# VectorE's rotation of the next query split in two, with the mask and the carry of the states between its cosine and its sine products

## What is computed

```
q = rope(x wq), k = rope(x wk), v = x wv          # 16 query heads, 4 key heads, 128 wide, batch 2
rope(t) = t * cos + rot(t) * sin                  # rot swaps the halves of a head
scores = (q k^T) * diag                           # within a block, with decay exp(-lam * distance)
o      = scores v + (q * q_dec) state             # what earlier blocks add, through the state
state  = blk * state + (k * k_dec)^T v            # carried from block to block
x      = x + (o wo)
```

## Time and profile before

| | us |
|---|---|
| median of 3 runs | 578.29 |
| lowest and highest | 576.17, 578.62 |
| the profiled execution | 576.15 (span of its core 574.5) |

### The profile page before, as it was taken

One profiled execution on the slowest core, in us unless ns is written; L12 is line 12 of the kernel. 1 busy time (PEld: TensorE's weight loads), 2 busy tenths in 40 slices (PEclk: granted clock), 3 DMA queues, 4 the chain that ended last, 5 costly groups with the idle time before them and its releaser, 6 DMA issues.

```text
span 574.5 us, 10574 instructions
## 1 busy us (share of the span) xinstructions
PE 503.9 (88%) x3560; PEld 449.3 (78%) x3560; DVE 337.2 (59%) x974; ACT 153.6 (27%) x381; POOL 290.3 (51%) x312
## 2 busy tenths in 40 slices
PE   8689999999378999899999999999878999999900
PEld 7589988886357989799989988889777898888700
DVE  6844444443367898977767868676674444444417
ACT  4102222222332233333233322332310222222211
POOL 0045666664337566557555645555004566666332
PEclk9879999999588999999999999999977999999965
DMA  7989997873722331212121212211495422877455
GB/s 232 331 255 314 347 335 278 286 244 109 251 93 66 92 111 56 67 54 84 51 78 50 81 56 83 61 51 47 135 343 181 140 93 92 293 261 238 144 207 192
DMA packets 54722, 93.10 MB, mean 162 GB/s; under 512 B 7424, under 2 KB 37376, under 8 KB 54656
## 3 DMA queue, kind: packets, MB, share of 16 engines
q1 hardware_dynamic: 45440, 71.29, 38.0%
q0 software_dynamic: 6912, 18.88, 10.0%
q10 hardware_dynamic: 2304, 2.10, 1.1%
HBM read 79.67 MB, written 12.58 MB: 161 GB/s over the span
## 4 chain that ended last, share of the span: by engine, by line
PE 69%; DVE 15%; issue 6%; DMA 6%; POOL 2%; ACT 1%; SPq 0%; DVEq 0%; ACTq 0%; POOLq 0%
PE bank L1196 11%; PE bank L1191 8%; PE bank L1291 7%; PE bank L1342 7%; PE bank L1215 5%; PE bank L1217 5%; PE bank L1324 4%; PE bank L1302 4%; PE bank L1313 3%; PE bank L1330 3%; PE bank L1163 3%; DVE x_sb L982 3%; PE bank L1256 2%; DMA shared<-z_dram 2%; PE bank L1206 1%
## 5 line engine op out<-in xcount | busy, mean ns | idle before, releaser
L492 POOL DMA_INDIRECT decay_all<-xn_dram,ids x72 | 69.6, 966 | 113.7 <-PE bank L1163 46.3
L938 DVE COPY oT_all<-bank 128x256 f32<-128x256 f32 x72 | 30.6, 425 | 126.2 <-PE bank L1163 126.2
L501 POOL DMA_INDIRECT z_dram<-probs_all,dest x72 | 70.2, 974 | 36.5 <-ACT probs_all L691 32.8
L564 POOL TENSOR_TENSOR shared<-shared 128x512 f32<-128x512 f32 x40 | 51.3, 1282 | 47.3 <-DVE shared L999 47.3
L1196 PE MATMUL bank<-w_ch_sb,oT_all 128*128 128x256 f32 x256 | 65.7, 379 | 0.0
L1291 PE MATMUL bank<-split_sb 128*128 128x512 f32 x240 | 64.2, 404 | 0.0
L683 ACT ACTIVATE rot<-bank 128x224 f32<-128x224 f32 x72 | 25.7, 357 | 127.1 <-PE bank L1196 127.1
L1191 PE MATMUL bank<-w_exp_sb,oT_all 128*128 128x192 f32 x256 | 53.2, 330 | 2.9 <-issue 1.6
L1342 PE MATMUL bank<-split_sb 128*128 128x256 f32 x384 | 53.5, 289 | 2.4 <-DVE split_sb L1022 2.3
L1191 PEld LDWEIGHTS bank<-w_exp_sb,oT_all 128*128 128x128 f32 x256 | 44.0, 189 | 9.6 <-issue 4.7
L1092 PE MATMUL bank<-idle_ones 128*128 128x128 f32 x244 | 39.5, 337 | 12.2 <-DMA shared<-z_dram 11.0
(11 more groups left out here) (146 smaller groups left out, 983.4 us busy)
## 6 DMA issues: line engine op xcount, KB each, us to landing
shared<-w_up_piece SPq DMA_DIRECT2D x32, 448.0 KB, 6.0
w_exp_sb<-w_exp SPq DMA_DIRECT2D x32, 384.0 KB, 7.3
shared<-w_down_piece SPq DMA_DIRECT2D x32, 256.0 KB, 4.3
w_ch_sb<-w_ch SPq DMA_DIRECT2D x16, 384.0 KB, 6.3
shared<-z_dram SPq DMA_DIRECT2D x8, 512.0 KB, 5.3
wq_all<-wq SPq DMA_DIRECT2D x32, 128.0 KB, 2.1
decay_all<-decay SPq DMA_DIRECT2D x32, 128.0 KB, 2.1
wo_all<-wo SPq DMA_DIRECT2D x32, 128.0 KB, 2.1
```

Of the source, the lines that this page charges most:

```text
L492: pool.indirect_dma_start(out=xg[s], out_offset=None, in_=xn_dram[l][:, :], in_offset=bass.IndirectOffsetOnAxis(ap=ids[:, SEQ[t]:SEQ[t] + ...
L501: pool.indirect_dma_start(out=z_dram[l][:, :], out_offset=bass.IndirectOffsetOnAxis(ap=dest[:, SEQ[t]:SEQ[t] + 1], axis=0), in_=y_sb[s], i ...
L564: nc.gpsimd.tensor_tensor(dst, rope_a[r % 2], rope_b[r % 2], ALU.add).then_inc(roped, 1)
L938: nc.vector.tensor_copy(xgT[s], xT_ps[s][:, 0:D].rearrange("p (k t) -> p k t", k=KD)).then_inc(xgT_ready[s], 1)
```

## The change

`rotate` gets a second argument. With "cos" it issues the cosine product alone, with "sin" the two sine products alone (its waits for the projection and for `roped` are written in both), and without it the whole. VectorE's loop calls it with "cos" for the next query where the whole call stood, and with "sin" behind the carry of the states. The key's rotation and the rotations ahead of the loop stay whole. Nothing is added or removed but these waits, and no other engine's code changes.

```diff
-            def rotate(p):
+            def rotate(p, part="whole"):
...
-                nc.vector.tensor_tensor(rope_a[r % 2], ps[:, :], cos_sb, ALU.mult)
+                if part != "sin":
+                    nc.vector.tensor_tensor(rope_a[r % 2], ps[:, :], cos_sb, ALU.mult)
+                if part == "cos":
+                    return
...
                 for p in projections(n, "query"):
-                    rotate(p)
+                    rotate(p, "cos")
                 mask(n)
                 carry(n)
+                for p in projections(n, "query"):
+                    rotate(p, "sin")
                 for p in projections(n, "behind"):
                     rotate(p)
```

## The result

The changed kernel takes 581.48 us (median of 13 runs, 578.47 to 584.88), the kernel before 578.07 (13 runs beside them, 574.17 to 581.33): a ratio of **1.006, 95% interval 1.0034 to 1.0087**. It is slower, by 2 to 5 us. Forecast were 577.7 us, and 574.3 to 581.3 as the range.

A forecast was written before the change was run, and what follows sets the result against it. TensorE was taken to bound the attention, VectorE the crowded units 3 to 8. Gains of 1.7 us outside that stretch and 1.1 lost in it gave -0.6 us: 577.7 us, range 574.3 to 581.3.

The forecast's parts named there:

- The quiet unit: Units 12, 28, 29 and 30: earlier mask shortens each from 6.19 to 5.94 us, .25 gained each, 1.0 in all.
- Unit 19: Unit behind a key rotation and row statistics, 6.91 us long: the earlier mask clears its .65 us idle, .65 gained.
- Units 3 and 7: Late-sum units: unit 3's products start at 200.82 instead of 201.40, without their mask wait; unit 7 wins .75 us.
- Pair 5-6: Longer late sum holds unit 6's output projection; the pair takes 16.67 us instead of 15.58, 1.09 lost.
- margin of `rope_read`: Quiet unit: this signal comes at 394.30, the projection that needs it could start at 394.49, leaving .19 us.
- The rival of the late sine products: Units with m = 0 or 3: sine products .3 us beyond the margin delay projections, 583.6 us (.1 beyond: 580.8); chance .17.
- the first rival (the port doesn't matter): Units 3 to 8: GpSimd costs the late sums nothing new, TensorE's free 3.6 us goes too, 573.0 us; chance .13.
- held mask: Rival: mask held until its old time, quiet gains go and crowded losses stay, 579.8 us (+1.5); chance .08.
- the crowded stretch: Units 3 to 8, with the late sums: GpSimd's instructions lengthen them; .41 + 1.09 - .38 = 1.1 us lost.
- Normalisation to 202.5, ahead of GpSimd's sum: Unit 3 step: after sine products to 202.11, normalisation ends at 202.5; GpSimd's sum runs from 202.4 to 203.65.
- unit 30: Counted among the quiet units: the earlier mask gains .25 us there.
- the ring: Scores, states, carry, sine, GpSimd's sum, next scores: some 5.5 us against a unit of 5.94, margins above zero.

The follow-up runs named there:

- e5: Changed kernel with each of a late sum's four instructions replaced by a one-input bn_stats, leaving out the late sums: 575.56 us, ratio to before 0.9961.
- e12: e5 with the four normalisations of the late tiles also replaced by a bn_stats: 574.10 us in a single execution, beside 578.23 for the kernel before.
- e6: Changed kernel with the cosine product also behind mask and carry, except units 1, 3, 5, 7 and 30 (whole rotation ahead): 577.35 us, ratio to before 0.9989.
- e4b: Changed kernel with 10 and 13 calls of unread matmuls ahead of the output projections in units 4 and 8: 580.14 us, ratio to before 1.0044.
- e2: Changed kernel with the rotation whole in units 1, 3, 5, 7 and 30, split in the others: 574.33 us, ratio to before 0.9948.

## Why the prediction was wrong

**Right.** The bound and the places of the gaps. The quiet unit: 5.93 to 5.94 us at 12, 28 and 29, as worked out. Unit 19: 6.26. Units 3 and 7: 6.3. Pair 5-6: 1.21 lost, 1.09 forecast. The mechanism of the loss, GpSimd's instructions beside those that read only SBUF, and its effect on the output projections of units 4, 6 and 8; e5 and e12 show it. That a margin of `rope_read` is left in a quiet unit: .19 worked out, .1 to .16 by e6, and this closely by two errors that cancel (the mask starts .14 behind the shown end of the scores, not .04, and the projection needs .05 behind the sine product, not .15). The rival of the late sine products did not happen; the first rival (the port doesn't matter) is refuted by e5. That the range's upper end, 581.3, lies near the measured 581.48 is no merit: it was put there for late sine products and a held mask, neither of which came. The price of the held mask, 1.5 us, was also not worked out: by the prediction's own figures 1.1 and the gains of units 3 and 7 (.66 and .75) would make 2.5.

**Wrong: the sum of the crowded stretch, +1.1 forecast, +5.0 measured.** Its steps, with what the runs showed:
- *The slow clock was not in the sum at all.* I let a wait of TensorE grow from .2 and .8 us to 2 and more and charged the wait alone. At 2.6 and 3.0 us of near idleness the clock fell, and the next 3 us ran at half speed: 1.5 us at each of two places, 3.1 in all (e4b brings back 1.2 at each, the rest then goes into the wait for the sine products). This is the largest term, and its size was in no row of before, since no such wait stood there; but the profile of the kernel before shows granted clocks of .5 and .8 where the first stage ends and the attention starts, from 144 to 187 us (40 slices of 14.4 us, in tenths), and that should have been a warning for a step that makes a gap:

```profile
PEclk9879999999588999999999999999977999999965
```

- *"Normalisation to 202.5, ahead of GpSimd's sum".* It started .05 us ahead and still ended .15 behind it, after 1.49 us instead of .41. Start in the record doesn't decide who goes first. With a late sum a little shorter than I put it (3.55, not 3.95), the output projection of unit 4 started .59 us later than worked out.
- Against that stand .38 us in unit 4: the wait for `rope_read` at its end that I charged was covered by the slow products.
  Unit 4: .59 + 1.52 - .38 = 1.73, which is 2.14 - .41. In units 7 and 8, 1.68 + .38 = 2.06 were missed: 1.55 is the clock, and .51 is the remainder, the port less the covered wait. The prediction gives no start for the output projection there, so these two can't be told apart.

**Wrong: unit 30.** I counted it among the quiet units, .25 us won. Behind it no projection stands between the sine products and the next scores, so the ring that I had named (sine, GpSimd's sum, scores) was bare there: .86 us lost (e2).

**Sum by the runs.** +5.0 in units 3 to 8, -1.5 in units 12, 19, 20, 24, 28 and 29, +.9 in unit 30: 4.4 us. That is the trace's difference. Unit 1's start differs by 1.2 us between the two profiled executions, ahead of anything that the change touches, and makes most of the rest of 5.9. The chances: slower by over .5% had .15; it deserved more, because every uncertain term of the crowded stretch (order at the port, clock) could only add.

The rule that the Trainium skill gives ("SBUF — State Buffer", section "Who interferes with whom": two SBUF inputs on VectorE contend with GpSimd's reads, one input outside the two-port modes doesn't) fits what e5 shows: 1.80 for 3.55 us. The normalisation has only one tensor as input, so the half of the rule on two inputs doesn't cover it; by the rule it would have to run in a two-port mode, and no run here shows in which mode it ran. What e12 shows is its time: .43 for 1.49. By the section's words for the one that is blocked the sum would have been 2 us higher; of the 3.9 us missed, 3.1 belong to the clock, .7 to the port less the covered waits, and .1 to units 5 and 6. That the first to issue goes first is not what the starts in the record show here.

## What to carry to other kernels

Moving an instruction moves what its signal starts: before sending a step later, list what the engine that it releases will then run beside. A wait that grows on TensorE to the lengths seen here (2.6 and 3.0 us) must be priced twice, as the wait and as the slow clock behind it. And an order that repeats should be worked at its last turn and at its most crowded one as well as at the typical one: here 26 of 30 units were forecast to a few hundredths, and units 4, 6, 8 and 30 decided; the same split without units 1, 3, 5, 7 and 30 gains .5% (e2).

## What the runs showed of the hardware that was not expected

- A VectorE `tensor_scalar` over 128x256 that starts .05 us ahead of a GpSimd instruction of 1.29 us ends .15 us behind it (1.49 instead of .41 us); a `bn_stats` in the same place takes .43.
- TensorE's granted clock was .50 in the 3.1 us behind 2.6 us with .24 us of matmuls in them; behind .84 and 1.28 us of idleness it stayed at 1.00. With matmuls on constants in the gap it stayed at 1.00 too (e4b).
- Undisturbed units of 6 to 9.5 us repeat to .03 us between kernels, while whole executions of the changed kernel scatter by over 1% (578.47 to 584.88 us).
